# Causal half of a gated attention block: 64 by 64 score tiles, and the next unit's normalisation spread over three engines

## The chip, the cores and the metric

The kernel runs on one core of one Trainium2 chip. The metric is the device time of one execution in microseconds (us); of several executions the median is given. Engines are called TensorE (PE in the rows, PEld its weight loads), VectorE (DVE), ScalarE (ACT), GpSimd (POOL) and SyncE (SP, whose queue SPq issues most transfers).

## The reference, cut to what matters

Inputs are x and a context, both 32 sequences of 128 tokens by 128 features, and weights. There are 16 heads of 8 features.

```python
x = x + tanh(g_x) * attention(layernorm(x), ctx, ctx)          # plain, "x half"
x = x + tanh(g_f) * ffn(layernorm(x))                          # "causal half" and last stage
# ffn(x): with q_in = k_in = rope(x), v_in = x
q, k, v = q_in @ Wq.T + bq, k_in @ Wk.T + bk, v_in @ Wv.T + bv
scores  = where(causal, q @ k.T * scale, -inf)
attn    = softmax(scores) @ v
x1      = layer_norm(x + attn @ Wo.T + bo)                      # the reference adds bo here
moe     = two best of eight experts, gated
return layer_norm(x1 + moe)
```

The first residual, x plus gated attention, is itself normalised and goes through the second attention, whose scores are causally masked.

## The kernel before, in words

**Tiling.** Two sequences make a unit, so there are 16 units of the x half (u = 0 to 15) and 16 of the causal half (u = 16 to 31). One tile of scores holds 4 heads of one sequence, 128 queries by 4 times 128 keys; 4 tiles make a sequence and 8 a unit. The tiles are numbered n = 0 to 255, the causal ones from 128. Every head's query and key features stand split in bf16 parts in 64 partitions of qk: even tiles read partitions 0 to 63, odd ones 64 to 127 (the row half).

**Two kinds of scores.** Each tile is computed twice. The first kind (s_bank, queries in the output's partitions) serves only for the row maximum, which VectorE takes (line 618). GpSimd splits the maxima of a sequence in three bf16 parts (max_split, line 294), TensorE transposes them (line 440), ScalarE copies them (line 522) and sends them into a row of qk by a transfer. The second kind (st_bank, keys in the partitions) is computed 13 tiles later (LAG), has the maximum already subtracted, and goes through ScalarE's exponential (line 515) into the product with the values (av, line 432, four 128 by 32 tiles, each in two passes as the data are float32).

**Order of the work.** Each engine runs one hand-written loop over the same slots n, in which s = n // 8 counts units and t = n % 8 the slot of the unit; what it does in a slot is fixed by the tests on s and t. Nothing is reordered at run time: an engine that waits holds back all that stands behind it. In slot n TensorE does, in this order: the transposition of maxima where n - 6 is a multiple of 4 (t = 2 and 6), the scores of tile n and of tile n - 13, the value product of tile n - 15, the transposition of an attention output (t = 0 and 4), and preparation for unit s + 2: transposed inputs at t = 0 (line 357), query and key projections at t = 2 (lines 362, 363), value projection at t = 5 (line 368). Tiles n and n - 13 are in opposite row halves, so that their instructions are issued in turn. s_bank and st_bank have two buffers each: tile n waits for the maximum of tile n - 2.

**Masking before.** For causal tiles the function triangle (line 372) first writes a mask to the whole bank in two matmuls (blocks 0 and 1 of each head). The stationary operand is esel, a 64 by 128 slice that puts a 64-row mask on half of the output partitions and zero on the other; the 4 products of line 385 then accumulate onto it, each with a 64 by 128 stationary operand and 128 moving columns. The block of queries 0 to 63 and keys 64 to 127 is masked by constant rows in qk.

**Preparation of a causal unit before.** In slot t = 1 of unit s VectorE takes the statistics of x for unit s + 3 (lines 574, 577). In slot t = 2 GpSimd computes the reciprocal deviation (lines 242, 244) and normalises both rows, one instruction for each sequence (line 249); in slots 3 to 6 it applies the rotary embedding in four steps (lines 267, 271 twice, 277), with max_split of slot 4 in between. For unit s + 2 it adds the output bias to the normalised rows in slot 1 (line 281), makes the middle bf16 part of queries and keys in slot 6 (line 286) and the low part in slot 7 (line 291). ScalarE makes the high part in slot 3 (line 493) and VectorE the rest in slot 4 (line 599).

**Constants.** SyncE loads the later constants between the units' transfers: two in each of s = 0 to 8, five in each of s = 9 and 10 (later_constants, line 180). Four of these 28 transfers are esel (line 198).

**Last stage.** After the attention of all units comes a separate stage (output projection, experts, last normalisation), which the change leaves as it is.

Of the kernel before, what the change touches and what calls it, by code (L numbers as in the profile page):

```python
# [7 lines left out]
ALU = mybir.AluOpType  # L8
# [5 lines left out]
P = 128  # L14
# [28 lines left out]
AHEAD = 4  # L43
LATER = 28
LATE_STEP = 12
# [5 lines left out]
def gated_block_kernel(nc, x, ctx_in, g_x, g_f, wq_t, wk_t, wv_t, wo_t, bq, bk, bv, bo,  # L51
# [3 lines left out]
    with es:  # L55
# [8 lines left out]
        idb = sb("idb", [P, P], BF16)  # L64
        esel = sb("esel", [P, 2, P], BF16)
        mqk = sb("mqk", [P, P], BF16)
# [24 lines left out]
        stats = [sb(f"stats{i}", [P, G, 6]) for i in range(2)]; mv = [sb(f"mv{i}", [P, G, 2]) for i in range(2)]  # L91
        ve = sb("ve", [P, G]); rstd = sb("rstd", [P, G])
        xp = [sb(f"xp{i}", [P, G, P]) for i in range(2)]; cp = [sb(f"cp{i}", [P, G, P]) for i in range(2)]
# [28 lines left out]

        stat = sem("stats"); rstd_s = sem("rstd_steps"); ln = sem("ln_applied"); perm = sem("context_permuted")
        rope = sem("rope_steps"); vx = sem("x_values"); vy = sem("y_values")
# [33 lines left out]
        def high_parts(u):  # L158
            return u + 1 if u < GROUPS else 2 * (u + 1) - GROUPS

        def row(sp, dst, src, semaphore):
# [18 lines left out]
        def later_constants(sp, first, end):  # L180
            whole = ((mqk, mask_qk), (mkq, mask_kq), (wq, wq_t), (wk, wk_t),
                     (wv, wv_t), (wo, wo_t), (gwt, gate_t), (ewt, exp_t), (ebs, exp_b),
                     (cost, cos_t), (sint, sin_t))
            rows = ((bvb, bv), (bob, bo), (gbb, gate_b), (l1w, ln1w), (l1b, ln1b), (l2w, ln2w), (l2b, ln2b))
            columns = ((l1wc, ln1w), (l1bc, ln1b))
            for i in range(first, end):
                if i < 11:
                    dst, src = whole[i]
                    sp.dma_start(dst[:, :], src).then_inc(c_late, 16)
                elif i < 18:  # L190
                    dst, src = rows[i - 11]
                    row(sp, dst[:, :], src, c_late)
                elif i < 20:
                    dst, src = columns[i - 18]
                    sp.dma_start(dst[:, :], src.rearrange("(n o) -> n o", o=1)).then_inc(c_late, 16)
                elif i < 24:
                    half, block = divmod(i - 20, 2)
                    sp.dma_start(esel[64 * half:64 * half + 64, block, :],
                                 identb[64 * block:64 * block + 64, :]).then_inc(c_late, 16)
                elif i < LATER:  # L200
                    half, k = divmod(i - 24, 2)
# [13 lines left out]
        def sp_attention(sp):  # L215
            for s in range(FIRST_SLOT // TILES, UNITS):
                u = s + 2
                if 0 <= u < UNITS:
                    if u >= RING:
                        sp.wait_ge(st, (u - RING + 1) * TILES)  # L220
                    sp.dma_start(qk[u % RING][SLOTS:P:8, :, 0, :], qrow[in_y(u)][:, :]).then_inc(stk[u % RING], 16)
                    sp.wait_ge(h0_s, high_parts(u))
                    stack_parts(sp, u, 0)
                    if u >= 1:
                        sp.wait_ge(h1_s, u + 1)
                        stack_parts(sp, u, 1)
                    sp.wait_ge(h2_s, u + 1)
                    stack_parts(sp, u, 2)
                if AHEAD <= s + 7 < GROUPS:
                    load_inputs(sp, s + 7)  # L230
                if 0 <= s <= 8:
                    later_constants(sp, 2 * s, 2 * s + 2)
                elif 9 <= s <= 10:
                    later_constants(sp, 5 * s - 27, 5 * s - 22)

        def pool_attention(pool):
            def normalised(u):
                pool.wait_ge(stat, (u + 1) * 4)
                if in_x(u - 1):
                    pool.wait_ge(ln, u * G)  # L240
                by = 1.0 / SCALE ** 2 if in_x(u) else 1.0
                pool.tensor_scalar(ve[:, :], mv[u % 2][:, :, 1], by, EPS * by, ALU.mult, ALU.add).then_inc(rstd_s, 1)
                pool.wait_ge(rstd_s, u * 2 + 1)
                pool.tensor_tensor(rstd[:, :], ve[:, :], mhalf[:, :], ALU.pow).then_inc(rstd_s, 1)  # L244
                pool.wait_ge(rstd_s, u * 2 + 2)
                if in_x(u):
                    return
# [11 lines left out]
            def rotate(u, step):  # L259
# [54 lines left out]
            for n in range(FIRST_SLOT, END_SLOT):  # L314
# [7 lines left out]
                if q is not None and q < B:  # L322
                    add_residual(q)
                if in_y(s + 3):
                    if t == 2:
                        normalised(s + 3)
                    if 3 <= t <= 6:
                        rotate(s + 3, t - 3)
                if in_y(s + 2) and t == 1:
                    add_attention_bias(s + 2)  # L330
                if 0 <= s + 2 < UNITS:
                    if t == (4 if in_x(s + 2) else 6):
                        middle_part(s + 2)
                    if t == (5 if in_x(s + 2) else 7):
                        low_part(s + 2)
                if in_x(s + 3):
                    if t == 5:
                        normalised(s + 3)
                    if t == 6:
# [3 lines left out]
        def pe_attention(pe):  # L343
# [34 lines left out]
            def product(bank, n, j, keys_first):  # L378
# [4 lines left out]
                k = qk[u % RING][rows, HEADS * r + j, 1, b * P:(b + 1) * P]  # L383
                masked = in_y(u)
                return pe.matmul(bank[:, j * P:(j + 1) * P], k if keys_first else q, q if keys_first else k,  # L385
                                 start=not masked, stop=True, skip_group_check=masked)

            def scores(n, m):
# [19 lines left out]
                for j in range(HEADS):  # L408
                    if n is not None:
                        ins = product(s_bank[n % 2], n, j, False)  # L410
                        if j == HEADS - 1:
                            ins.then_inc(sc, 1)
                    if m is not None:
                        ins = product(st_bank[m % 2], m, j, True)
                        if j == HEADS - 1:
# [149 lines left out]
        def dve_attention(dve):  # L565
            def statistics(u):
# [4 lines left out]
                if u >= 2:  # L571
                    dve.wait_ge(ln, (u - 1) * G)
                for b in range(G):
# [5 lines left out]
            def normalised(u):  # L579
# [3 lines left out]
                for b in range(G):  # L583
                    dve.tensor_scalar(xp[u % 2][:, b, :].rearrange("q (x hs) -> q x hs", hs=HS),
                                      one(x_all, u * G + b).rearrange("q (hs x) -> q x hs", hs=HS),
                                      mv[u % 2][:, b, 0:1], rstd[:, b:b + 1],
                                      ALU.subtract, ALU.mult).then_inc(ln, 1)

            def rest_of_high(u):
# [49 lines left out]
            for n in range(FIRST_SLOT, END_SLOT):  # L639
# [515 lines left out]
```

## Time and profile before

| what | value |
|---|---|
| runs | 498.08 us median of 3 (497.17 to 498.41) |
| the profiled execution | 498.87 us, span of its instructions 497.1 us |
| mean granted TensorE clock | 0.973 |
| busy TensorE, VectorE, ScalarE, GpSimd | 437.8, 381.9, 276.5, 326.3 us |
| first masked tile, last tile of the first kind | 162.6 us, 331.2 us |
| end of attention, start of the last stage | about 346 us |

Span and execution differ by what lies around the first and last instruction. Busy time of TensorE counts overlapping matmuls once, and includes the time in which a result is still on its way to the bank, so its share is no measure of how full it is.

### The profile page before, as it was taken

The page shows a single profiled execution, that of the slowest core. Times are in us where ns is not written, and L with a number is a line of the kernel's source. Part 1 is how long each engine was busy: PE and PEld are TensorE (multiplying, and loading weights), DVE is VectorE, ACT ScalarE, POOL GpSimd, SP SyncE. Part 2 cuts the span into 40 slices and gives each one's busy share as a digit, 9 for nine tenths or more (in the row PEclk, how much of TensorE's full clock was granted, in tenths as well). Part 3 has the DMA queues.
Part 4 walks back from the last instruction along what each step waited for, and adds up shares of the span by engine and source line. Part 5 has one row for each costly group of instructions (what it writes and reads, how often), then busy time and mean ns, then how long its engine had stood idle before and what let it go on. Part 6 is the DMA issues. An engine that isn't in the chain of part 4 may idle for free.

```text
span 497.1 us, 15905 instructions
## 1 busy us (share of the span) xinstructions
PE 437.8 (88%) x5728; PEld 274.9 (55%) x5728; DVE 381.9 (77%) x1189; ACT 276.5 (56%) x693; POOL 326.3 (66%) x704
## 2 busy tenths in 40 slices
PE   0479888889888999999999999998799999999983
PEld 0245444545444666666666666665466666667552
DVE  5788999999877777777767676861568999999981
ACT  1136767676765666566566566666245545454540
POOL 5465767676689988788888877320327676767654
PEclk9999999999889999999999999999699999999995
DMA  7866785854633334443433444300000000000000
GB/s 163 188 157 156 191 186 137 190 136 109 152 94 94 91 86 114 113 99 89 103 86 90 104 101 121 87 11 6 1 0 12 23 11 23 16 19 22 13 21 21
DMA packets 88333, 42.70 MB, mean 86 GB/s; under 512 B 16312, under 2 KB 88128, under 8 KB 88256
## 3 DMA queue, kind: packets, MB, share of 16 engines
q1 hardware_dynamic: 77392, 38.93, 32.3%
q10 hardware_dynamic: 10864, 2.76, 2.6%
q8 instruction: 46, 0.75, 0.7%
q14 instruction: 31, 0.25, 0.2%
HBM read 5.75 MB, written 2.10 MB: 16 GB/s over the span
## 4 chain that ended last, share of the span: by engine, by line
PE 39%; DVE 29%; POOL 15%; issue 8%; ACT 4%; DMA 1%; ACTq 1%; SPq 1%; POOLq 0%; DVEq 0%
PE u_bank L432 8%; DVE nm L618 7%; PE s_bank L385 6%; PE s_bank L375 5%; DVE z_acc L949 5%; POOL xn_all L249 4%; PE t_bank L357 4%; PE u_bank L445 2%; PE s_bank L779 2%; PE u_bank L800 2%; DVE stats L574 2%; POOL rstd L244 2%; PE st_bank L779 2%; POOL rc L267 2%; POOL z_rstd_ L677 1%
## 5 line engine op out<-in xcount | busy, mean ns | idle before, releaser
L618 DVE TENSOR_REDUCE nm<-s_bank 128x4 f32<-128x512 f32 x256 | 173.3, 684 | 56.0 <-PE s_bank L385 55.4
L515 ACT ACTIVATE pt<-st_bank 128x512 f32<-128x512 f32 x256 | 151.2, 601 | 85.8 <-PE st_bank L385 44.2
L432 PE MATMUL u_bank<-pt,vaug 128*32 128x128 f32 x2048 | 110.9, 289 | 1.6 <-DVE ao L635 0.3
L385 PE MATMUL s_bank<-qk 64*128 64x128 bf16 x1024 | 102.4, 225 | 11.2 <-DVE nm L618 6.2
L385 PE MATMUL st_bank<-qk 64*128 64x128 bf16 x1024 | 102.5, 221 | 0.0
L385 PEld LDWEIGHTS s_bank<-qk 64*128 64x128 bf16 x1024 | 68.9, 97 | 38.9 <-issue 18.8
L385 PEld LDWEIGHTS st_bank<-qk 64*128 64x128 bf16 x1024 | 69.0, 95 | 0.4
L432 PEld LDWEIGHTS u_bank<-pt,vaug 128*32 128x32 f32 x2048 | 41.1, 109 | 29.6 <-issue 4.8
L375 PE MATMUL s_bank<-mqk,esel 64*128 64x256 bf16 x256 | 49.7, 274 | 0.6 <-DVE nm L618 0.4
L375 PE MATMUL st_bank<-mkq,esel 64*128 64x256 bf16 x256 | 49.7, 274 | 0.0
L291 POOL TENSOR_TENSOR part<-r,part 128x512 bf16<-128x512 f32 x32 | 37.1, 1159 | 2.6
L864 ACT ACTIVATE z_gated<-s_bank,z_gates 128x128 f32<-128x128 f32 x64 | 18.3, 368 | 35.7 <-PE u_bank L800 35.7
L800 PE MATMUL u_bank<-z_gated,idf 128*128 128x128 f32 x256 | 38.0, 293 | 0.0
L779 PE MATMUL s_bank<-ewt,z_x_t 128*128 128x512 f32 x64 | 36.1, 647 | 0.4 <-DVE z_acc L949 0.4
L302 POOL TENSOR_SCALAR mst<-nm 128x16 bf16<-128x16 f32 x64 | 13.2, 206 | 35.2 <-DVE nm L618 35.2
L522 ACT ACTIVATE mts<-m_bank 128x128 bf16<-128x128 bf16 x64 | 17.8, 278 | 29.4 <-PE m_bank L440 29.4
L800 PEld LDWEIGHTS u_bank<-z_gated,idf 128*128 128x128 f32 x256 | 31.8, 195 | 4.0 <-issue 0.2
L779 PE MATMUL st_bank<-ewt,z_x_t 128*128 128x512 f32 x64 | 33.6, 607 | 0.0
L445 PE MATMUL u_bank<-idf,us 128*128 128x128 f32 x128 | 28.1, 302 | 4.9 <-ACT us L531 4.9
L675 POOL TENSOR_SCALAR z_ve<-z_mv 128x2 f32<-128x2 f32 x16 | 3.1, 193 | 43.9 <-DVE z_mv L893 43.8
L375 PEld LDWEIGHTS s_bank<-mqk,esel 64*128 64x128 bf16 x256 | 14.2, 94 | 22.8 <-issue 16.6
L249 POOL TENSOR_SCALAR xn_all<-x_all,mv,rstd 128x128 f32<-128x128 f32 x32 | 25.4, 798 | 1.8
(120 smaller groups left out, 884.0 us busy)
## 6 DMA issues: line engine op xcount, KB each, us to landing
qk<-part SPq DMA_DIRECT2D x221, 128.0 KB, 2.7
x_all<-x SPq DMA_DIRECT2D x16, 128.0 KB, 2.7
qk<-qrow SPq DMA_DIRECT2D x32, 64.0 KB, 2.2
qk<-mts ACTq DMA_DIRECT2D x64, 32.0 KB, 2.6
out<-z_o SPq DMA_DIRECT2D x16, 128.0 KB, 1.8
c_all<-ctx_in SPq DMA_DIRECT2D x14, 128.0 KB, 3.1
ewt<-exp_t SPq DMA_DIRECT2D x1, 512.0 KB
qk<-part ACTq DMA_DIRECT2D x3, 128.0 KB, 2.8
```

The lines of the kernel that those rows point to most:

```text
L249: pool.tensor_scalar(one(xn2_all, u * G + b), one(x_all, u * G + b), mv[u % 2][:, b, 0:1], rstd[:, b:b + 1], ALU.subtract, ALU.mult).then_ ...
L291: pool.tensor_tensor(part[u % 2][:, 2:2 * PARTS:PARTS, :], r32[:, :].rearrange("c (o t) -> c o t", o=2), part[u % 2][:, 1:2 * PARTS:PARTS, ...
L357: ins = pe.transpose(t_bank[:, i * P:(i + 1) * P], a, idf[:, :])
L375: pe.matmul(to, esel[rows, block, :], mask[rows, rows].unsqueeze(1).broadcast_to([64, HEADS, 64]), start=block == 0, stop=False, skip_grou ...
L385: return pe.matmul(bank[:, j * P:(j + 1) * P], k if keys_first else q, q if keys_first else k, start=not masked, stop=True, skip_group_che ...
L432: ins = pe.matmul(u_bank[b][32 * j:32 * j + 32, r * P:(r + 1) * P], v, pt[m % 4][:, j, :], start=half == 0, stop=half == 1, skip_group_che ...
L445: ins = pe.transpose(u_bank[q % 2][:, W + r * P:W + (r + 1) * P], us[q % 2][:, r * P:(r + 1) * P], idf[:, :])
L515: act.activation(pt[m % 4][:, :, :].rearrange("k j q -> k (j q)"), st_bank[m % 2][:, :], ACT.Exp).then_inc(ex, 1)
L618: dve.tensor_reduce(nm[q % 2][:, first:first + HEADS], s_bank[n % 2][:, :].rearrange("q (j k) -> q j k", j=HEADS), AX_X, ALU.max, negate=T ...
L779: ins = pe.matmul(e_bank[b][k][:, :], zx1t[i][:, b * P:(b + 1) * P], ewt[:, k * 512:(k + 1) * 512], start=True, stop=True)
L800: ins = pe.matmul(dst, idf[:, :], zyg[:, b, e, :], start=False, stop=e == HALF - 1)
L949: dve.scalar_tensor_tensor(out=zacc[i][e % 2][:, b, :], in0=e_bank[b][0][:, e * P:(e + 1) * P], scalar=zg[i][:, b, e:e + 1], in1=zacc[i][( ...
```

## The change

1. Score tiles of the causal half, both kinds, are computed in quarters: output partitions 0 to 63 and 64 to 127 by separate matmuls with a 64 by 64 stationary operand. The 4 products of a kind become 8. The two mask matmuls of a kind stay two, but each now writes only its own 64 partitions and 64 columns of each head; the identity itself is their stationary operand, and esel with its 4 transfers is gone (LATER 28 to 24; s = 9 and 10 load three constants each instead of five). In the 13 slots after n = 255 the second kind is alone and is in quarters too.
2. VectorE's statistics of a causal unit move from slot 1 of unit u - 3 to slot 5 of unit u - 4, and GpSimd's deviation from slot 2 of u - 3 to slot 7 of u - 4. ve and rstd get a second buffer.
3. Of the two rows of a unit VectorE normalises the first (slot 1, behind a maximum and the division of an attention output) and GpSimd the second (slot 1).
4. On GpSimd the rotary steps move to slots 1 (step 0), 2 (steps 1 and 2) and 5 (step 3), the output bias from slot 1 to slot 3, the middle and low parts of causal units from slots 6 and 7 to 5 and 6.

```diff
-LATER = 28
+LATER = 24
-                elif i < 24:
-                    half, block = divmod(i - 20, 2)
-                    sp.dma_start(esel[64 * half:64 * half + 64, block, :],
-                                 identb[64 * block:64 * block + 64, :]).then_inc(c_late, 16)
...
-            def normalised(u):
+            def deviation(u):
                 pool.wait_ge(stat, (u + 1) * 4)
-                if in_x(u - 1):
-                    pool.wait_ge(ln, u * G)
+                if u >= 2:
+                    pool.wait_ge(ln, rows_done(u - 2))
...
-                for b in range(G):
-                    pool.tensor_scalar(one(xn2_all, u * G + b), one(x_all, u * G + b), mv[u % 2][:, b, 0:1],
-                                       rstd[:, b:b + 1], ALU.subtract, ALU.mult).then_inc(ln, 1)
+            def second_row(u):
+                pool.wait_ge(rstd_s, u * 2 + 2)
+                pool.tensor_scalar(one(xn2_all, u * G + 1), one(x_all, u * G + 1), mv[u % 2][:, 1, 0:1],
+                                   rstd[u % 2][:, 1:2], ALU.subtract, ALU.mult).then_inc(ln2, 1)
...
                 if step == 0:
-                    pool.wait_ge(ln, (u + 1) * G)
+                    pool.wait_ge(ln, rows_done(u))
+                    pool.wait_ge(ln2, u - GROUPS + 1)
...
                 if in_y(s + 3):
+                    if t == 1:
+                        second_row(s + 3)
+                        rotate(s + 3, 0)
                     if t == 2:
-                        normalised(s + 3)
-                    if 3 <= t <= 6:
-                        rotate(s + 3, t - 3)
-                if in_y(s + 2) and t == 1:
+                        rotate(s + 3, 1)
+                        rotate(s + 3, 2)
+                if 0 <= s + 2 < UNITS:
+                    if t == (4 if in_x(s + 2) else 5):
+                        middle_part(s + 2)
+                    if t == (5 if in_x(s + 2) else 6):
+                        low_part(s + 2)
+                if in_y(s + 2) and t == 3:
                     add_attention_bias(s + 2)
-                if 0 <= s + 2 < UNITS:
-                    if t == (4 if in_x(s + 2) else 6):
-                        middle_part(s + 2)
-                    if t == (5 if in_x(s + 2) else 7):
-                        low_part(s + 2)
+                if in_y(s + 3) and t == 5:
+                    rotate(s + 3, 3)
+                if in_y(s + 4) and t == 7:
+                    deviation(s + 4)
...
-                to = bank[:, :].rearrange("p (j k) -> p j k", j=HEADS)[:, :, 64 * block:64 * block + 64]
-                pe.matmul(to, esel[rows, block, :], mask[rows, rows].unsqueeze(1).broadcast_to([64, HEADS, 64]),
-                          start=block == 0, stop=False, skip_group_check=True)
+                outs = slice(64 * block, 64 * block + 64)
+                to = bank[outs, :].rearrange("p (j k) -> p j k", j=HEADS)[:, :, outs]
+                pe.matmul(to, idb[rows, rows], mask[rows, rows].unsqueeze(1).broadcast_to([64, HEADS, 64]),
+                          start=True, stop=False, skip_group_check=True)
...
-                return pe.matmul(bank[:, j * P:(j + 1) * P], k if keys_first else q, q if keys_first else k,
-                                 start=not masked, stop=True, skip_group_check=masked)
+                for outs in (slice(0, 64), slice(64, P)) if quarters else (slice(0, P),):
+                    ins = pe.matmul(to[outs, :], fixed[:, outs], moving,
+                                    start=not masked, stop=True, skip_group_check=masked)
+                return ins
...
+                quarters = n is None or mask_n
...
+            def first_row(u):
+                dve.wait_ge(rstd_s, u * 2 + 2)
+                dve.tensor_scalar(one(xn2_all, u * G), one(x_all, u * G), mv[u % 2][:, 0, 0:1],
+                                  rstd[u % 2][:, 0:1], ALU.subtract, ALU.mult).then_inc(ln, 1)
...
+                if in_y(s + 4) and t == 5:
+                    statistics(s + 4)
                 if in_y(s + 3) and t == 1:
-                    statistics(s + 3)
+                    first_row(s + 3)
```

rows_done(u) is (u + 1) * 2 up to the last x unit and grows by one for each causal unit.

## Rows read from the trace of the kernel before

**Rows 1.** The page, busy time of each engine
```profile
PE 437.8 (88%) x5728; PEld 274.9 (55%) x5728; DVE 381.9 (77%) x1189; ACT 276.5 (56%) x693; POOL 326.3 (66%) x704
```

**Rows 2.** Windows, causal units: from and to, PE, PEld, DVE, ACT, POOL, clock, DMA, GB/s
```profile
182.00:313.90 131.90, 128.32 (x2147) 82.89 (x2149) 96.31 (x227) 82.00 (x182) 106.50 (x229) 1.00 0.41 99
```

**Rows 3.** Chain that ended last, one causal unit: start us, us, what
```profile
295.32 0.44 PE t_bank L357 x4
...
297.44 0.48 DVE stats L574 x2
...
298.56 0.72 POOL rstd L244
...
299.39 1.58 POOL xn_all L249 x2
...
301.06 0.74 POOL rc L267
...
302.93 0.23 PE m_bank L440
...
308.71 0.63 PE t_bank L362 x2
309.34 0.43 PE t_bank L363 x2
```

**Rows 4.** Groups of lines, GpSimd, 182 to 313.9 us: busy us, mean ns, idle before
```profile
L249 POOL TENSOR_SCALAR xn_all<-x_all,mv,rstd 128x128 f32<-128x128 f32 x22 | 17.4, 799 | 1.2
...
L242 POOL TENSOR_SCALAR ve<-mv 128x2 f32<-128x2 f32 x11 | 2.1, 193 | 10.4 <-DVE mv L577 10.4
```

**Rows 5.** Timeline, VectorE, 318 to 334 us, two maxima four slots apart
```profile
321.53 0.69 DVE L618 TENSOR_REDUCE nm<-s_bank 128x4 f32<-128x512 f32 x1 [0.58 <-PE s_bank L385]
...
325.68 0.69 DVE L618 TENSOR_REDUCE nm<-s_bank 128x4 f32<-128x512 f32 x1 [0.58 <-PE s_bank L385]
```

**Rows 6.** Timeline, TensorE, one masked slot and the next one's first matmul
```profile
303.99 0.28 PE L375 MATMUL s_bank<-mqk,esel 64*128 64x256 bf16 x1
...
304.11 0.27 PE L375 MATMUL s_bank<-mqk,esel 64*128 64x256 bf16 x1
...
304.22 0.22 PE L385 MATMUL s_bank<-qk 64*128 64x128 bf16 x1
...
304.39 0.22 PE L385 MATMUL s_bank<-qk 64*128 64x128 bf16 x1
...
304.54 0.43 PE L432 MATMUL u_bank<-pt,vaug 128*32 128x128 f32 x8
...
304.90 0.28 PE L375 MATMUL s_bank<-mqk,esel 64*128 64x256 bf16 x1
```

**Rows 7.** Lines 375, 432, 767: count, ns min/median/max, first and last start
```profile
L375 PE MATMUL s_bank<-mqk,esel x256: 266/269/280, 162.6 to 331.3; 64*128 64x256 bf16 x128
...
L432 PE MATMUL u_bank<-pt,vaug x2048: 269/297/422, 34.6 to 345.8; 128*32 128x128 f32 x187
...
L767 PEld LDWEIGHTS u_bank<-gwt,z_x_t x64: 186/192/333, 354.3 to 475.1; 128*128 128x128 f32 x64
```

**Rows 8.** Timeline around the value projection of one causal unit
```profile
300.59 0.49 ACT L493 ACTIVATE part<-t_bank,bks 128x256 bf16<-128x256 f32 x1
...
301.51 0.48 DVE L599 SCALAR_TENSOR_TENSOR r<-t_bank,bks,part 128x256 f32<-128x256 f32 x1
...
302.05 0.52 PEld L368 LDWEIGHTS t_bank<-wv,txr 128*128 128x128 f32 x4 [0.37 <-DVE r L599]
302.05 0.71 PE L368 MATMUL t_bank<-wv,txr 128*128 128x128 f32 x4
```

**Rows 9.** Groups of lines, VectorE, 40 to 124 us
```profile
L584 DVE TENSOR_SCALAR xp<-x_all,mv,rstd 128x128 f32<-128x128 f32 x20 | 6.9, 388 | 0.0
```

**Rows 10.** Timelines of SyncE's queue (two rows) and TensorE, start of unit s = 13
```profile
108.88 1.83 SPq L198 DMA_DIRECT2D esel<-identb  x3
...
117.23 0.61 SPq L198 DMA_DIRECT2D esel<-identb  x1
...
130.27 0.23 PE L385 MATMUL s_bank<-qk 64*128 64x128 bf16 x1 [1.43 <-DMA qk<-part]
```

More of the change, by code:

```diff
@@ L64, in gated_block_kernel @@
         idb = sb("idb", [P, P], BF16)
-        esel = sb("esel", [P, 2, P], BF16)
         mqk = sb("mqk", [P, P], BF16)
@@ L91, in gated_block_kernel @@
         stats = [sb(f"stats{i}", [P, G, 6]) for i in range(2)]; mv = [sb(f"mv{i}", [P, G, 2]) for i in range(2)]
-        ve = sb("ve", [P, G]); rstd = sb("rstd", [P, G])
+        ve = [sb(f"ve{i}", [P, G]) for i in range(2)]; rstd = [sb(f"rstd{i}", [P, G]) for i in range(2)]
         xp = [sb(f"xp{i}", [P, G, P]) for i in range(2)]; cp = [sb(f"cp{i}", [P, G, P]) for i in range(2)]
@@ L195, in later_constants @@
                     sp.dma_start(dst[:, :], src.rearrange("(n o) -> n o", o=1)).then_inc(c_late, 16)
-                elif i < 24:
-                    half, block = divmod(i - 20, 2)
-                    sp.dma_start(esel[64 * half:64 * half + 64, block, :],
-                                 identb[64 * block:64 * block + 64, :]).then_inc(c_late, 16)
                 elif i < LATER:
-                    half, k = divmod(i - 24, 2)
+                    half, k = divmod(i - 20, 2)
                     dst, src = ((bqs, bq), (bks, bk))[k]
@@ L324, in pool_attention @@
                 if in_y(s + 3):
+                    if t == 1:
+                        second_row(s + 3)
+                        rotate(s + 3, 0)
                     if t == 2:
-                        normalised(s + 3)
-                    if 3 <= t <= 6:
-                        rotate(s + 3, t - 3)
-                if in_y(s + 2) and t == 1:
-                    add_attention_bias(s + 2)
-                if 0 <= s + 2 < UNITS:
-                    if t == (4 if in_x(s + 2) else 6):
-                        middle_part(s + 2)
-                    if t == (5 if in_x(s + 2) else 7):
-                        low_part(s + 2)
+                        rotate(s + 3, 1)
[6 more added lines that the diff above has]
+                if in_y(s + 2) and t == 3:
+                    add_attention_bias(s + 2)
+                if in_y(s + 3) and t == 5:
+                    rotate(s + 3, 3)
+                if in_y(s + 4) and t == 7:
+                    deviation(s + 4)
                 if in_x(s + 3):
                     if t == 5:
-                        normalised(s + 3)
+                        deviation(s + 3)
                     if t == 6:
@@ L373, in triangle, with product @@
                 rows = slice(64 * half, 64 * half + 64)
-                to = bank[:, :].rearrange("p (j k) -> p j k", j=HEADS)[:, :, 64 * block:64 * block + 64]
-                pe.matmul(to, esel[rows, block, :], mask[rows, rows].unsqueeze(1).broadcast_to([64, HEADS, 64]),
-                          start=block == 0, stop=False, skip_group_check=True)
-            def product(bank, n, j, keys_first):
+                outs = slice(64 * block, 64 * block + 64)
+                to = bank[outs, :].rearrange("p (j k) -> p j k", j=HEADS)[:, :, outs]
+                pe.matmul(to, idb[rows, rows], mask[rows, rows].unsqueeze(1).broadcast_to([64, HEADS, 64]),
+                          start=True, stop=False, skip_group_check=True)
+            def product(bank, n, j, keys_first, quarters):
                 u, t = divmod(n, TILES)
@@ L383, in product @@
                 k = qk[u % RING][rows, HEADS * r + j, 1, b * P:(b + 1) * P]
+                fixed, moving = (k, q) if keys_first else (q, k)
+                to = bank[:, j * P:(j + 1) * P]
                 masked = in_y(u)
-                return pe.matmul(bank[:, j * P:(j + 1) * P], k if keys_first else q, q if keys_first else k,
-                                 start=not masked, stop=True, skip_group_check=masked)
+                for outs in (slice(0, 64), slice(64, P)) if quarters else (slice(0, P),):
+                    ins = pe.matmul(to[outs, :], fixed[:, outs], moving,
+                                    start=not masked, stop=True, skip_group_check=masked)
+                return ins
             def scores(n, m):
@@ L409, in scores @@
                     if n is not None:
-                        ins = product(s_bank[n % 2], n, j, False)
+                        ins = product(s_bank[n % 2], n, j, False, quarters)
                         if j == HEADS - 1:
@@ L413, in scores @@
                     if m is not None:
-                        ins = product(st_bank[m % 2], m, j, True)
+                        ins = product(st_bank[m % 2], m, j, True, quarters)
                         if j == HEADS - 1:
@@ L571, in statistics @@
                 if u >= 2:
-                    dve.wait_ge(ln, (u - 1) * G)
+                    dve.wait_ge(ln, rows_done(u - 2))
+                if in_y(u - 2):
+                    dve.wait_ge(ln2, u - 2 - GROUPS + 1)
                 for b in range(G):
```

15 lines of the change are left out of this document (8 added, 7 removed).

## The prediction

> **What bounds the kernel now.** The page comes first. TensorE is busy for 88% of the span and no other engine for more than 77% [rows 1], which suggests TensorE but does not prove it, since matmul records overlap. The windows of the causal half say the same: 128.3 of 131.9 us for TensorE, 106.5 for GpSimd, 96.3 for VectorE, all at full granted clock [rows 2]. The chain that ended last shows more. In each causal unit it runs along TensorE for half of the unit, then through VectorE's statistics, GpSimd's deviation, both normalised rows and the first rotary step, then max_split of slot 4, and comes back to TensorE at the transposed maxima of slot 6 [rows 3]. This loop closes once per unit: the statistics stand behind VectorE's maximum of slot 1, which needs TensorE's slot 1, and TensorE's slot 6 needs GpSimd's maxima, which stand behind the rows. So the unit's length is that of the loop.
>
> The length: the first masked tile starts at 162.6 us [rows 7]; 13 units later, at s = 29, the next one starts its slot 0 near 304.9 us, after the slots of [rows 6]. That makes 142.3 / 13 = 10.94 us per unit.
>
> How much of that does TensorE need by itself? Late in the half there is nothing to prepare, and two maxima four slots apart are 325.68 - 321.53 = 4.15 us apart [rows 5], with VectorE idle before both: TensorE paces this stretch. A unit is two of these, 8.30 us. The preparation adds 0.44 (transposed inputs), 0.63 + 0.43 (projections) [rows 3] and 0.71 (values) [rows 8]: 10.49 us. So TensorE waits for about 0.45 us per unit, and the loop is only just the bound. Whoever frees the loop alone wins 0.45 us per unit at most; the rest has to come from TensorE's own work.
>
> **The score tiles.** In a masked slot the first mask matmul starts at 303.99, the second 0.12 us later, the first product 0.11 after that, the last one 0.17 further (three steps of 0.055), the value product at 304.54, the next slot at 304.90: 0.90 us in all [rows 6]. The rows of st_bank beside them start a few ns later, so the two row halves already run beside each other. The change leaves the 128 streamed columns of a product as they are but needs two products for each head, and it writes the two mask blocks to different output partitions. If all four quarters run side by side, one mask step of 0.11 us disappears and the products take four steps as now. Are column parts of the array seen to work side by side? The value product is the nearest case: its eight matmuls on four column parts take 0.43 us from first start to last end, of which the last one's own record is 0.27 [rows 6, 7]. So eight start within 0.16 us, although two in succession on one part need about 0.11. Four parts do overlap.
>
> What is exposed grows, however. The first mask matmul of a slot has a record of 280 ns against 269 for the second, so about 10 ns of its weight load shows today. The first value matmuls have 297 against 272 (the last one's 0.27), 25 ns for 32 columns [rows 7]. By proportion 64 columns loaded that way would show 50 ns: plus 40. Four parts instead of two start some 7 ns apart (0.05 of the 0.16 us over 7 starts), plus 15, and each later step may be a nanosecond or two longer. I take 0.11 - 0.04 - 0.02 = **0.05 us saved per slot**. The ends: 0.11 saved if nothing more is exposed; 0.22 lost if the two column halves of a row half take turns, that is, four product steps more at 0.055 with the mask unchanged. I stay near the first end, as the value product is the nearest row.
>
> The Trainium skill, TensorEngine Tiling (Array Packing), Restrictions and Gotchas, states that column tiling switches off the fast weight load. By TensorE: Matmul & The Clock Gate, LDWEIGHTS, a load of 64 columns would then take 53 ns as an estimate, just within a product's step; by this the sum stays as it is, and it names a reason for the 40 ns.
>
> **Statistics and rows.** GpSimd loses one instruction of 0.80 us per unit [rows 4], the second xn_all; VectorE gains one of 0.39, priced by the same operation in the x half [rows 9]. The statistics and the deviation are not cheaper, only earlier: GpSimd's wait before the deviation, 10.4 us over 11 units or 0.95 each [rows 4], goes, because in slot 7 the statistics of slot 5 are long done. Its new wait is the first rotary step for VectorE's row in slot 1; behind that wait stand the rest of the rotation, the bias and max_split of slot 4. From the start of TensorE's slot 1: 0.6 to VectorE's maximum, 0.6 for it, 0.55 for the division, 0.4 for the row, then on GpSimd 0.7 + 1.0 + 0.7 + 1.1 for the first step, the middle steps, the bias and max_split: 5.7. Then TensorE does slots 6, 7 and 0 with their extras, 3.5. That loop is 9.2 us long, shorter than TensorE's own 10.1. GpSimd's sum: 106.5 busy over 12.06 units is 8.8, plus about 0.65 of gaps between dependent small operations, less 0.8: 8.7. VectorE's: 8.0 plus 0.4. Neither binds. The bias in slot 3 waits for the transposed inputs of slot 0, which TensorE has done three slots earlier, so I cost it at nothing; it is hidden by the margin of the 9.2 us loop, and would cost its 0.73 us if that were gone. The earlier middle and low parts only bring transfers forward.
>
> What is late next is the value projection. It waits for VectorE's rest of slot 4, behind ScalarE's high part of slot 3. Today the rest ends at 301.99 and TensorE starts at 302.05, about 0.17 us after its slot 5 (0.90 long) was through [rows 6, 8]. That wait is timed from slot 3, and two slots shorter by 0.05 each reach it 0.1 us earlier, so it grows to 0.28 us.
>
> A causal unit then takes 10.49 - 8 x 0.05 + 0.28 = 10.37 us: 0.57 less, 7.4 us over 13 units.
>
> **The seam.** Units s = 13 to 15 have unmasked first tiles but already prepare causal units. They take 162.6 - 130.27 = 32.3 us, 10.8 each, by the same loop. With it gone GpSimd's sum binds: 8.7 plus two residual additions of 0.46, 9.6, with waits 9.9. Saved 2.7 us. At the start of s = 13 TensorE waits 1.43 us for the stacked parts [rows 10]. SyncE issued four transfers of esel ahead of them, 1.83 + 0.61 = 2.4 us of its time [rows 10]; without them I expect 1.2 of the 1.43 back. Its bounds are 0 (the transfer is late for another reason) and 1.43.
>
> **The rest.** Unit s = 29 has no row to make and takes 10.6; it gains 0.2. Units 30 and 31: 16 slots at 0.05, 0.8. The 13 slots of the second kind alone: 0.65. The last stage is untouched.
>
> **The sum.** 1.2 + 2.7 + 7.4 + 0.2 + 0.8 + 0.65 = 12.95. The profiled execution took 498.87 us: 485.9. The median of the runs is 0.8 lower: **485 us**.
>
> **The rivals.**
> - *Everything hides* (0.11 per slot): another 0.057 x 141 slots = 8 us, so 477. For it: the next slot's loads may start while the array empties. Against: the 25 ns of [rows 7] show after exactly such a change of shape. Chance 0.15.
> - *The loop closes again or the value projection's wait swallows the shorter slots*: the unit stays near 10.7, 13 x 0.33 = 4 us more, or slots gain nothing, 7 us more: 489 to 495. For it: margins of some tenths on four engines in fixed order. Chance 0.15.
> - *Slower: the quarters of one row half do not overlap, because each step's load waits for the matmul before it in those rows or for the other half's load.* Then a slot is 0.22 longer, 0.27 above my forecast, over 141 slots 38 us, less the wait that it hides, 3: 520. It decides from a slot about 0.04 us longer than today (13 us of gain over 141 slots is 0.09 above the forecast's slot); between, say at 0.1 longer, it gives 505. For it: a 128-column load with hardly any columns to stream has a record of 192 ns [rows 7], against 0.11 for 32 columns, so slow loads exist here. Against: the value product's four parts. A second way to the same end is supply: a slot holds 40 loads and matmuls now and 56 afterwards; if 0.90 / 40 were the fastest that instructions arrive, the slot would be 1.27. Nothing in the rows says that 0.90 is such a limit, as the starts inside a slot come 3 to 7 ns apart after a wait. Chance 0.16.
> - *No change within 0.3%*, gains and losses cancelling: 0.04.
>
> The Trainium skill, TensorE: Matmul & The Clock Gate, Packing small matmuls, has a rule for the slower rival: a load overlaps with matmuls in flight only when the row group differs. The trace disagrees for successive products of one row half, which start every 0.055 us, each with its own load.
>
> **Numbers.** The forecast, 480 to 489, has 0.50. 0.3% is 1.5 us, about what a measurement of this kernel can tell from no change. Faster by more: 0.50 + 0.15 + 0.15 = 0.80; within 0.04; slower 0.16. The range takes in the first rival and nearly all of the second, 475 to 497, and leaves out the slower one.
>
> **What would show it.** In the profile after: four mask matmuls starting within some 25 ns, then product steps of about 0.057; a masked slot of 0.85 and four slots 3.95 apart in the last units; no wait of GpSimd for mv; about 0.28 before line 368's load; causal units of 10.4; no wait of 1.4 us at s = 13. Product starts of a row half spread over 0.4 us would make the prediction wrong on the slow side; a slot below 0.82 on the fast side.

## The result and the profile after

The changed kernel takes 483.03 us (median of 4, 482.78 to 483.36) against 497.81 before in the same session: ratio 0.970, 95% interval 0.969 to 0.972. The forecast was 485 us, so against 497.81 the gain is 14.8 us where 12.8 would have met it.

The page of the changed kernel, busy time by engine, answers to [rows 1]:

```profile
PE 420.6 (87%) x6804; PEld 265.6 (55%) x6804; DVE 382.6 (80%) x1205; ACT 273.5 (57%) x693; POOL 313.5 (65%) x688
```

There are 1076 more matmuls and as many more loads, and TensorE is busy for 17 us less. VectorE did not get shorter; its share rose. One masked slot of the changed kernel, TensorE's timeline, answers to [rows 6]:

```profile
281.64 0.29 PE L381 MATMUL s_bank<-mqk,idb 64*64 64x256 bf16 x1
281.65 0.29 PE L381 MATMUL st_bank<-mkq,idb 64*64 64x256 bf16 x1
281.65 0.29 PE L381 MATMUL s_bank<-mqk,idb 64*64 64x256 bf16 x1
281.65 0.29 PE L381 MATMUL st_bank<-mkq,idb 64*64 64x256 bf16 x1
281.78 0.22 PE L394 MATMUL s_bank<-qk 64*64 64x128 bf16 x1
...
281.95 0.22 PE L394 MATMUL st_bank<-qk 64*64 64x128 bf16 x1
282.10 0.43 PE L443 MATMUL u_bank<-pt,vaug 128*32 128x128 f32 x8
282.46 0.23 PE L451 MATMUL m_bank<-idb,mst 128*128 128x128 bf16 x1
```

Four mask matmuls start within 0.01 us, the products follow 0.14 us later in four groups of four matmuls, 0.056 us from group to group, and from the first mask to what follows the value product it is 282.46 - 281.64 = 0.82 us, where it was 0.91 by the same rounding. The groups of the mask, and those of GpSimd and VectorE between 182 and 300 us, to be held against [rows 4, 7]:

```profile
L381 PE MATMUL s_bank<-mqk,idb x256: 266/293/293, 157.5 to 315.3; 64*64 64x256 bf16 x128
...
L247 POOL TENSOR_SCALAR xn_all<-x_all,mv,rstd 128x128 f32<-128x128 f32 x10 | 8.0, 801 | 0.0
L266 POOL TENSOR_TENSOR rc<-xn_all,cost 128x256 f32<-128x256 f32 x11 | 8.0, 726 | 8.8 <-DVE xn_all L604 8.8
L240 POOL TENSOR_SCALAR ve<-mv 128x2 f32<-128x2 f32 x10 | 1.9, 193 | 0.8
...
L604 DVE TENSOR_SCALAR xn_all<-x_all,mv,rstd 128x128 f32<-128x128 f32 x10 | 3.4, 336 | 0.0
```

A mask matmul's record is 293 ns, 24 above the 269 of one with nothing exposed; the forecast had 50. GpSimd's wait for mv is gone, and 8.8 us over 11 units stand in its place before the first rotary step, for VectorE's row. It costs nothing, as it is not on the chain of waits that ended last. One causal unit of that chain:

```profile
281.28 0.44 PE t_bank L362 x4
...
283.50 0.63 PE t_bank L367 x2
284.13 0.43 PE t_bank L368 x2
...
286.23 0.47 ACT part L504
...
286.73 0.89 DVE r L617 x2
...
287.66 0.71 PE t_bank L373 x4
...
291.43 0.44 PE t_bank L362 x4
```

No statistics, no row and no max_split are in it; it stays on TensorE except for the high part and the rest before the value projection, and for 0.12 us before slot 0. The loop of [rows 3] is open. The starts of the maximum of a unit's first tile give the lengths (timeline of VectorE, units 16 and 29; two rows of the changed kernel, then two of the kernel before):

```profile
158.20 0.68 DVE L636 TENSOR_REDUCE nm<-s_bank 128x4 f32<-128x512 f32 x1
...
290.74 0.69 DVE L636 TENSOR_REDUCE nm<-s_bank 128x4 f32<-128x512 f32 x1
...
163.25 0.69 DVE L618 TENSOR_REDUCE nm<-s_bank 128x4 f32<-128x512 f32 x1 [0.29 <-PE s_bank L385]
...
305.58 0.68 DVE L618 TENSOR_REDUCE nm<-s_bank 128x4 f32<-128x512 f32 x1
```

(290.74 - 158.20) / 13 = 10.20 us, against (305.58 - 163.25) / 13 = 10.95 before. Read at that instruction, the stages give this, in us:

| kernel | unit 12 | 13 to 15 | mean of 16 to 29 | 29 | 30 | median of runs |
|---|---|---|---|---|---|---|
| before | 9.70 | 32.6 | 10.95 | 10.56 | 8.26 | 497 to 498 |
| changed | 9.01 | 29.4 | 10.20 | 10.15 | 8.04 | 483.03 |
| quarters alone | 8.38 | 32.9 | 10.75 | 10.39 | 8.81 | 494.09 |
| schedule alone | 9.03 | 29.4 | 10.52 | 10.51 | 8.26 | 489.29 |
| masks in quarters, products whole | 9.02 | 29.4 | 10.60 | 10.58 | 8.39 | 491.18 |

"Mean of 16 to 29" is from the start of 16 to that of 29, 13 units. Of the 16.3 us between the two spans, 9.8 lie there, 3.1 in units 13 to 15 and 0.7 in unit 12. The spans differ by more than the medians (14.8), because the traced execution of the kernel before was a long one (498.87 us). About 1.2 us lies before unit 12, where the changed kernels differ among themselves by more (102.2 to 104.0 us for the same work), so it is not put down to the change.

### The profile page after: what moved, and what is told of

Its sections match the earlier page's. It is cut to its first block, busy times and chain, and to the rows that moved or that the text cites. A ratio compares the mean times of both kernels' runs of the same rounds, so it can differ in the third digit from the quotient of the medians.

```text
span 480.8 us, 18054 instructions
## 1 busy us (share of the span) xinstructions
PE 420.6 (87%) x6804; PEld 265.6 (55%) x6804; DVE 382.6 (80%) x1205; ACT 273.5 (57%) x693; POOL 313.5 (65%) x688
## 4 chain that ended last, share of the span: by engine, by line
PE 37%; DVE 18%; POOL 3%; ACT 2%; issue 2%; ACTq 0%; POOLq 0%; DVEq 0%
PE u_bank L443 8%; DVE z_acc L969 5%; PE s_bank L381 5%; PE s_bank L394 4%; PE s_bank L799 2%; PE u_bank L820 2%; DVE r L617 2%; PE st_bank L799 2%; PE t_bank L373 2%; POOL z_rstd_ L697 2%; PE t_bank L367 2%; PE u_bank L456 2%; PE st_bank L394 2%; DVE z_two L945 1%; DVE z_y L994 1%
## 5 line engine op out<-in xcount | busy, mean ns | idle before, releaser
L636 DVE TENSOR_REDUCE nm<-s_bank 128x4 f32<-128x512 f32 x256 | 171.5, 682 | 37.6 <-PE s_bank L394 34.6
L526 ACT ACTIVATE pt<-st_bank 128x512 f32<-128x512 f32 x256 | 149.1, 601 | 77.2 <-PE u_bank L443 41.1
L394 PE MATMUL s_bank<-qk 64*64 64x128 bf16 (+1 forms) x1536 | 102.5, 221 | 12.2 <-DVE nm L636 7.7
L394 PE MATMUL st_bank<-qk 64*64 64x128 bf16 (+1 forms) x1588 | 101.7, 218 | 0.0
L394 PEld LDWEIGHTS s_bank<-qk 64*64 64x64 bf16 (+1 forms) x1536 | 72.9, 104 | 36.1 <-issue 18.8
L394 PEld LDWEIGHTS st_bank<-qk 64*64 64x64 bf16 (+1 forms) x1588 | 72.1, 103 | 0.0
L381 PE MATMUL s_bank<-mqk,idb 64*64 64x256 bf16 x256 | 38.3, 291 | 2.7 <-ACT pt L526 0.8
L381 PE MATMUL st_bank<-mkq,idb 64*64 64x256 bf16 x256 | 38.3, 293 | 0.1
L381 PEld LDWEIGHTS s_bank<-mqk,idb 64*64 64x64 bf16 x256 | 14.5, 103 | 26.8 <-issue 18.4
L285 POOL TENSOR_SCALAR part<-r 128x512 bf16<-128x512 f32 x32 | 19.9, 620 | 13.4 <-DVE r L617 7.1
```

Source lines behind the costliest of these rows:

```text
L285: pool.tensor_scalar(part[u % 2][:, 1:2 * PARTS:PARTS, :], r32[:, :].rearrange("c (o t) -> c o t", o=2), 1.0, 0.0, ALU.mult, ALU.add).then ...
L381: pe.matmul(to, idb[rows, rows], mask[rows, rows].unsqueeze(1).broadcast_to([64, HEADS, 64]), start=True, stop=False, skip_group_check=True)
L394: ins = pe.matmul(to[outs, :], fixed[:, outs], moving, start=not masked, stop=True, skip_group_check=masked)
L526: act.activation(pt[m % 4][:, :, :].rearrange("k j q -> k (j q)"), st_bank[m % 2][:, :], ACT.Exp).then_inc(ex, 1)
L636: dve.tensor_reduce(nm[q % 2][:, first:first + HEADS], s_bank[n % 2][:, :].rearrange("q (j k) -> q j k", j=HEADS), AX_X, ALU.max, negate=T ...
```

## The experiments

In each edit, a line with a minus is the changed kernel's unless the text says otherwise. Each ratio is to the kernel before in the same session.

**1. Quarters alone,** on the kernel before.

```diff
 # kernel before, with triangle, product and scores of the changed kernel
-LATER = 28
+LATER = 24
```

> The kernel before with part 1 of the change alone (quarter tiles, esel and its transfers gone); the schedule of VectorE and GpSimd stays. Theory: before, the loop through statistics, rows and max_split sets the causal unit, and only four of TensorE's eight slots (6, 7, 0, 1) lie in it. A masked slot is 0.09 us shorter after the change, so a unit shrinks by 4 x 0.09 = 0.36 to about 10.6, 14 units give 5, the last two units 0.5, the 13 slots of the second kind 1.2, the seam at s = 13 up to 1.4: about 490 us. Rival (TensorE alone set the unit before): all eight slots count, 0.72 per unit, 10 us more for 14 units in place of 5: about 485.

Measured: 494.09 us, ratio 0.992 (0.990 to 0.994). Neither expectation was met: 3.9 us gained, where the theory had 8 and its rival 13. The unit is 0.20 shorter, not 0.36. The chain of waits still runs through the rows, and in slot 0, inside the loop, a new wait takes 0.11 us and stretches the mask by 0.05:

```profile
247.06 0.11 issue
247.17 0.27 PE s_bank L371
...
252.39 1.58 POOL xn_all L244 x2
254.05 0.73 POOL rc L262
```

(These are from its own chain of waits, slot 0 first and then the loop's GpSimd part.) Most of what the eight slots save is waited away. Where the kernel before waits 0.37, 0.36, 0.27 and 0.20 us (before the loads of the value projection, of the maxima of slots 6 and 2, and of slot 0), this one waits 0.57, 0.44, 0.34 and 0.35: 0.50 of 0.72 us per unit. This speaks for the loop, against "TensorE alone".

**2. Schedule alone.**

```diff
 # changed kernel, with triangle, product, scores and esel (LATER = 28) of the kernel before
```

> The changed kernel with whole tiles and esel as before (parts 2 to 4 of the change alone). Theory: the loop is gone, TensorE needs 10.49 us per causal unit and waits some 0.2 for the value projection: 10.7 in place of 10.94, 3 us over 13 units, and 2.7 to 3.5 in the three units before them, nothing at the transfers of esel: about 492 us. Rival (the loop was everything, the tiles little): about 486.

Measured: 489.29 us, ratio 0.983 (0.981 to 0.986). A causal unit takes 10.52 us, close to what was added up from [rows 3, 5, 8] as TensorE's own time. The theory's mechanism holds, but the gain that it expected was too small. 13 units give 0.43 each, 5.5 us instead of 3. The wait for the value projection is there, but the 10.52 already hold it. Its row in the last of these units, where 0.20 would be the plain distance:

```profile
291.70 0.41 PEld L378 LDWEIGHTS t_bank<-wv,txr 128*128 128x128 f32 x3 [0.37 <-DVE r L616]
```

So TensorE needs 10.52 - 0.17 = 10.35 us by itself, and the sum of row lengths was too long by about as much as this wait.

Alone, the two parts give 3.9 and 8.7 us, together 14.8. The 2 us between are about what the loop had kept of the quarters: in the 13 units they give 2.6 us under the old schedule and 4.3 under the new one.

**3. The esel transfers back,** under the new schedule and, in 11, under the old.

```diff
-LATER = 24
+LATER = 28
 # the four transfers of esel and five constants in s = 9 and 10 as before; nothing reads esel
```

> The changed kernel with the four transfers of esel back in their places in SyncE's queue; nothing reads esel. Theory: the wait of 1.43 us at the start of s = 13 was SyncE's queue and comes back in part: 1.2 us slower than the changed kernel, 484.2 us, with a wait for qk<-part at unit 13. Rival (the wait went because GpSimd's parts of unit 13 are ready earlier or for another reason): as the changed kernel, 483.0.

Measured: 483.36 us, ratio 0.971 (0.969 to 0.974), unit 12 at 9.02. The rival holds: no wait for qk<-part. In all kernels with the new schedule but run 8 unit 12 is 9.0 us rather than the 8.4 of run 1: VectorE's first early statistics stand there before the last maxima, and TensorE waits 0.78 us for a maximum where it waits 0.15 in run 1.

**4. Masks in quarters, products whole.**

```diff
-                quarters = n is None or mask_n
+                quarters = False
```

> The changed kernel with the masks in quarters and the products whole (64 by 128). Theory A: going from 64 by 64 to 64 by 128 tiles costs like the other changes of shape, in which about 0.09 us more than a plain step pass: the masked slot goes back to about 0.90 and the time to 483 + 141 x 0.09 minus what other waits hide, 493. Theory B: a change of columns alone costs nothing, and the products needn't be split: 483 or, as fewer loads are issued, a little less.

Measured: 491.18 us, ratio 0.986 (0.984 to 0.988). TensorE's timeline of one slot:

```profile
254.48 0.29 PE L381 MATMUL st_bank<-mkq,idb 64*64 64x256 bf16 x1
254.71 0.23 PE L394 MATMUL s_bank<-qk 64*128 64x128 bf16 x1
...
254.89 0.22 PE L394 MATMUL s_bank<-qk 64*128 64x128 bf16 x1
...
255.03 0.42 PE L443 MATMUL u_bank<-pt,vaug 128*32 128x128 f32 x8
255.39 0.23 PE L451 MATMUL m_bank<-idb,mst 128*128 128x128 bf16 x1
```

Theory A holds. Mask to product takes 0.23 us where quarters throughout take 0.14, so changing only the column width of the tiles costs 0.09 us. The mask step that was saved is used up by it: the slot takes 255.39 - 254.48 = 0.91 us, and four slots of the last units 4.21 against 4.15 before. The split products, whose step is no shorter (0.056 against 0.055), are what makes the split masks pay. No run splits the products alone.

**5. Both rows on GpSimd,** statistics still ahead.

```diff
-                pool.tensor_scalar(one(xn2_all, u * G + 1), ...).then_inc(ln2, 1)
+                for b in range(G):
+                    pool.tensor_scalar(one(xn2_all, u * G + b), ...).then_inc(ln2, 1)
...
-                if in_y(s + 3) and t == 1:
-                    first_row(s + 3)
```

> The changed kernel with both rows of a causal unit normalised on GpSimd in slot 1, as in the kernel before but with the statistics still a step ahead. Theory: with the statistics ahead the sharing is worth nothing, because GpSimd stands idle for 0.81 us before the first rotary step, waiting for VectorE's row, which is as long as the row takes on GpSimd (0.80): 483 us within 1. Rival (GpSimd's 0.80 us per unit was on the path and sharing it is what freed the loop): 0.4 to 0.8 us per unit more, 489 to 494.

Measured: 483.78 us, ratio 0.974 (0.973 to 0.976), against 0.971 (0.970 to 0.973) of run 6 in the same session. GpSimd's timeline shows the exchange, 1.58 us of rows with no wait after them:

```profile
273.82 1.58 POOL L250 TENSOR_SCALAR xn_all<-x_all,mv,rstd 128x128 f32<-128x128 f32 x2
275.49 0.72 POOL L268 TENSOR_TENSOR rc<-xn_all,cost 128x256 f32<-128x256 f32 x1
```

From unit 19 on it is as expected (10.15 for unit 29 in both). Units 14 and 15 take 10.64 and 10.45 instead of 10.08 and 10.03: with two residual additions more there GpSimd is the bound (busy for 19.55 of the 21.08 us), and the delay fades out only in units 16 to 18 (10.71, 10.45 and 10.41 instead of 10.28, 10.29 and 10.23). That is 1.8 us between the two traces, and 1 us between the medians of this run and run 6.

**6. The bias in slot 1.**

```diff
-                if in_y(s + 2) and t == 3:
+                if in_y(s + 2) and t == 1:
                     add_attention_bias(s + 2)
```

> The changed kernel with the output bias back in slot 1 of GpSimd, behind the first rotary step. Theory: in slot 1 and in slot 3 it stands between the same max_splits of slots 0 and 4, so nothing that TensorE waits for moves: 483.0 within 0.7. Rival (the place of the bias matters, since the rotary steps come later): 1 to 3 us slower.

Measured: 482.71 us, ratio 0.971 (0.970 to 0.973). The place between the two max_splits does not matter.

**7. The value projection in slot 6.**

```diff
-                    if t == 5:
+                    if t == 6:
                         project_v(s + 2)
```

> The changed kernel with the value projection in slot 6 in place of 5. Theory: TensorE's wait of 0.36 to 0.39 us for VectorE's rest before line 373 is the largest that is left in a causal unit and goes, as the rest is ready before slot 6 ends: 14 x 0.37 = 5 us, 478. Rival (another wait, VectorE's maxima or ScalarE's exponentials, takes its place): 481 to 483.

Measured: 480.18 us, ratio 0.967 (0.965 to 0.968). Between the two expectations. The wait before line 373 is gone, but a new one comes up before slot 0:

```profile
258.10 0.10 PEld L381 LDWEIGHTS s_bank<-mqk,idb 64*64 64x64 bf16 x1 [0.49 <-issue]
```

VectorE ends the maximum of tile 6 just before (it starts at 257.37, behind the statistics). The unit is 10.05 us.

**8. The exponential before the copy of the maxima.**

```diff
+                if 0 <= n - LAG < LAST_TILE:
+                    exp(n - LAG)
                 q = seq_at(n, 6)
                 if q is not None:
                     copy_max(q)
-                if 0 <= n - LAG < LAST_TILE:
-                    exp(n - LAG)
```

> The changed kernel with ScalarE's exponential ahead of the copy and transfer of the maxima in slots 2 and 6. Theory: the wait that the profile calls issue before slots 0 and 4 (0.36 in place of 0.20 before the mask's load) is for the exponential two tiles earlier, which stands behind ScalarE's issue of a transfer (0.54 us); with the exponential first it goes. Four slots of the last units take 4.02 us now, and would take 3.78 to 3.9; in a preparing unit up to 0.15 in slot 0. 14 x 0.13 + 4 x 0.15 = 2.5 us: 480.5. Rival (it is a wait for VectorE's maximum, as one row of the profile names it): 483.

Measured: 496.33 us, ratio 0.998 (0.997 to 0.999), 13 us slower than the changed kernel, and worse than both expectations. The diagnosis stood, the cure failed. Loads of TensorE in two slots of the last units:

```profile
319.27 0.10 PEld L381 LDWEIGHTS s_bank<-mqk,idb 64*64 64x64 bf16 x1 [0.20 <-issue]
320.09 0.10 PEld L381 LDWEIGHTS s_bank<-mqk,idb 64*64 64x64 bf16 x1 [0.20 <-issue]
321.43 0.20 PEld L456 LDWEIGHTS u_bank<-idf,us 128*128 128x128 f32 x2 [0.73 <-ACT us L542]
```

The 0.36 before slots 0 and 4 is back at 0.20, so ScalarE had held them. But the transfer's issue (0.54 us, 0.65 until ScalarE's next start) now stands right before slot 3's exponential and the copy of the attention output, whose transposition waits 0.53 more. The x half is longer too: its first 12 units take 108.6 us instead of some 103.

**9 and 10. The statistics in slot 2,** alone and with the value projection in slot 6.

```diff
-                if in_y(s + 4) and t == 5:
+                if in_y(s + 4) and t == (5 if s + 4 == GROUPS else 2):
                     statistics(s + 4)
```

> The changed kernel with the statistics of causal units from the second on in slot 2 in place of 5, where VectorE stands idle for 0.81 us while TensorE projects. Theory: in the changed kernel TensorE's slot 0 is held by ScalarE and the value projection by VectorE's rest, not by the statistics, so this alone brings little: 482 to 483. Rival (the statistics in slot 5 hold slot 0 already): 0.15 us per unit, 481 or less.

> The same, and the value projection in slot 6. With the projection alone moved, the unit was 10.05 and TensorE waited 0.3 before slot 0 for VectorE's maximum behind the statistics. Theory: with the statistics out of the way that wait goes too and the unit comes to 9.8, TensorE's own 9.77: 478 in the same session in which the projection alone gives 480. Rival (ScalarE's exponentials take the wait's place): 480, no gain.

Measured: alone 482.62 us, ratio 0.970 (0.967 to 0.973), no gain; with the projection moved **478.68 us**, ratio 0.962 (0.959 to 0.965), the best version found. Its interval lies below that of the changed kernel (0.969 to 0.972). Before the value projection and slot 0 only the plain 0.20 stands, and the unit takes 9.87 us; what is late next is max_split of slot 0, which GpSimd ends 0.16 us after TensorE could use it:

```profile
256.25 0.52 PEld L373 LDWEIGHTS t_bank<-wv,txr 128*128 128x128 f32 x4 [0.20 <-issue]
...
257.70 0.10 PEld L381 LDWEIGHTS s_bank<-mqk,idb 64*64 64x64 bf16 x1 [0.20 <-issue]
...
260.30 0.10 PEld L451 LDWEIGHTS m_bank<-idb,mst 128*128 128x128 bf16 x1 [0.36 <-POOL mst L307]
```

**11. Quarters alone, with esel's transfers still made.**

```diff
 # kernel before, with triangle, product and scores of the changed kernel; LATER stays 28
```

> Quarter tiles on the kernel before, with the four transfers of esel still made (nothing reads them). Theory: under the old schedule the transfers cause the wait of 1.4 us at the start of unit 13, since without them unit 12 took 8.38 in place of 9.70: unit 12 is 9.7 again, and of that some 0.6 comes back in unit 13: 495 us in place of 494. Rival (the wait at unit 13 depends on where the transfers of the x half happen to stand, not on esel): unit 12 stays at 8.4 and 494.

Measured: 494.23 us, ratio 0.993 (0.991 to 0.996), as without the transfers, and unit 12 again 8.38. The wait of 1.43 us in [rows 10] was in the one execution of before that was traced; with the same transfers it is in none of three other kernels (runs 2, 3 and 11). What caused it there stays open.

## Why the prediction was right

- **The loop.** Right, and its size too. TensorE's floor was forecast as 10.49 us (the four terms and 8.30 in fact add up to 10.51) and measured as 10.52 with the loop open and the old tiles, a wait of 0.17 included (run 2). That the loop over the engines, and not TensorE's work alone, set the unit is shown by run 1.
- **The slot.** The mechanism was right, two terms were mis-sized. Forecast 0.11 - 0.04 - 0.02 = 0.05 saved; measured 0.09, nearer to the 0.11 of the rival in which everything hides. The exposed load was scaled from 25 ns for 32 columns in float32 [rows 7] to 50 for 64 in bf16, but measured 24, 14 more than before rather than 40. Four tiles start within 0.01 us, where 0.015 was allowed for their stagger. The slower rival is out: both column halves start together, and 56 loads and matmuls pass in a slot of 0.82 us.
- **The load of 64 columns.** A product step is 0.056 us with loads of 64 columns, against 0.055 with 128. The estimate of 53 ns, which the prediction worked out from TensorE: Matmul & The Clock Gate, LDWEIGHTS, of the Trainium skill, fits in such a step.
- **Why 485 held although the slot was off.** This is partly luck. Eight slots at 0.09 instead of 0.05 would have taken another 0.32 us off a unit, and two waits gave part of that back. The value projection was named rightly as what is late next, but at 0.28 us. The loads of TensorE at the end of a unit of the changed kernel show 0.56 before line 373 and 0.36 before slot 0, where 0.20 is plain (run 10):

```profile
287.66 0.52 PEld L373 LDWEIGHTS t_bank<-wv,txr 128*128 128x128 f32 x4 [0.56 <-DVE r L617]
...
290.14 0.10 PEld L381 LDWEIGHTS s_bank<-mqk,idb 64*64 64x64 bf16 x1 [0.36 <-issue]
```

  So the first wait is 0.36 us, since the slots became shorter than forecast. The second, 0.16 us, was in no term; it is for ScalarE's exponential (run 8) and was not there before. With the floor of 10.35 from run 2 the unit comes to 10.35 - 0.72 + 0.36 + 0.16 = 10.15 us, as measured. The forecast's own sum with the measured slot and the first wait, 10.49 - 0.72 + 0.36 = 10.13, is as near only because its floor held 0.16 too much. The last units are the same case: four slots were forecast 3.95 us apart and are 3.97, because 4.15 - 4 x 0.09 gets the 0.16 before one slot in four on top.
- **The rows and the bias.** Sharing the rows is worth nothing in the later causal units and 1 to 2 us in units 14 to 18 (run 5). The prediction had charged it to the sum of GpSimd, where it belongs, but only for three units. The bias was rightly costed at nothing (run 6).
- **The seam.** Units 13 to 15 gave 3.1 us for 2.7. The 1.2 us for esel's transfers failed (runs 3 and 11): a wait seen once was taken for a property of the kernel. Most of that sum came back by chance, since unit 12 did get 0.7 shorter against the traced execution. The prediction also put the whole length of these units before down to the loop, but the clock was not full there. Windows of 3 us with TensorE's busy time, its granted clock, the share of the DMA engines and their GB/s, two of the kernel before, one of run 11 and one of the changed kernel:

```profile
132.00:135.00 3.00, 3.00 (x37) 0.51 0.77 191
138.00:141.00 3.00, 2.48 (x39) 0.64 0.23 53
...
141.00:144.00 3.00, 3.00 (x30) 0.50 0.72 183
...
138.00:141.00 3.00, 2.71 (x48) 1.00 0.66 184
```

  In all three kernels with the old schedule (before, runs 1 and 11) the clock falls to 1.2 GHz for a time between 132 and 149 us, just after waits of TensorE of 1.2 to 1.6 us; in none of the ten with the new one does it fall there. In run 11 it stayed low for 10 us, and unit 14 took 12.77 us where run 1, whose clock was back by then, has 10.57. How much of the 32.6 us before is due to it was not separated.
- **The end.** The 13 slots alone, forecast at 0.65 us, gave 1.0, but 0.8 us went again in the last stage, below.

## What to carry to other kernels

When an engine looks 97% busy, as TensorE did here, add up what it needs by itself in a stretch with nothing else to do; the difference to the measured period is the most that opening a loop can give, and shortening its work inside the loop gives only the part that lies in the loop. The split tiles paid here only when masks and products, all that stands between two changes of shape, took the same split. Where a wait was removed, the next one was within tenths of a microsecond: moving the statistics gained nothing by itself, moving the value projection 2 to 3 us, and both together 4. And a wait that one trace shows is to be looked for in a second one before a gain is built on it.

## What was not expected of the hardware

- Going from 64 by 64 tiles to 64 by 128 costs 0.09 us (run 4), though rows, banks and the data type stay. That is as much as between quite different shapes: from the last product to the value product 0.15 us pass, from product to product 0.055 [rows 6].
- A load of 64 columns in a column-split bf16 matmul exposes 24 ns (293 against 269), as much as one of 32 columns in float32 (25).
- The last stage began 17.0 us earlier (347.63 - 330.65), yet only 16.3 of it reached the end. Two windows of the trace of the changed kernel, with the busy time of TensorE, its granted clock, the share of the DMA engines and their GB/s:

```profile
330.00:333.00 3.00, 1.31 (x5) 0.66 0.00 0
333.00:336.00 3.00, 2.21 (x9) 0.50 0.00 0
```

In the kernel before the clock reads 1.00 for 347 to 350 us and 0.58 for 350 to 353. TensorE waits for other engines there in both, and its clock falls from 2.4 to 1.2 GHz, in the changed kernel 0.3 us after the stage's start and in the kernel before 2.9 us after it. The chains of waits show what that costs, first the changed kernel's, then the one before:

```profile
331.21 0.67 PE t_bank L761 x2
...
332.35 1.23 PE m_bank L771 x4
...
348.19 0.42 PE t_bank L741 x2
...
349.07 0.72 PE m_bank L751 x4
```

That is 0.25 + 0.51 = 0.76 us, about the 0.7 that went missing. It is hardly the change's doing. Over the traces of all thirteen kernels, which have the same last stage, the fall comes 0.3 to 3.4 us after the stage's start. In the kernel of run 10, which has the change too, it comes 3.0 us after it, and the stage takes 149.3 us where the changed kernel has 150.2. Why the clock falls sooner in some executions stays open.
